# A decoder layer on one core: side steps in four units instead of three, some additions moved to GpSimd, and four score matmuls ahead of a key tile's maxima

## What is computed

```python
x = x + self_attention(layernorm(x))             # 2 heads of 64, rotary, causal
x = x + cross_attention(layernorm(x), context)   # 16 heads of 8, 1601 keys per batch element
x = x + feed_forward(layernorm(x))               # 128 -> 512 -> 128, exact gelu

def feed_forward(x, W1, b1, W2, b2, scale):      # per batch element
    lt = x[1:17]; even, odd = lt[::2], lt[1::2]
    m1 = (even[:4, :, None] * odd[:4, None, :]).reshape(512, 128)
    m2 = (even[4:, :, None] * odd[4:, None, :]).reshape(128, 512)
    h = gelu(x @ (W1 + scale * m1).T + b1)
    return h @ (W2 + scale * m2).T + b2
```

## Time and profile before

| | us |
|---|---|
| median of 3 runs | 508.89 |
| the profiled execution | 505.43 |
| its span, first to last instruction | 503.4 |
| TensorE busy | 412.4 (82%) |
| VectorE busy | 351.8 (70%) |
| ScalarE busy | 299.2 (59%) |
| GpSimd busy | 58.7 (12%) |
| mean granted TensorE clock | 0.875 of full |

### The profile page before, as it was taken

How to read it: one execution, slowest core, us unless ns; L and a number is a source line. 1 busy time by engine, 2 the same in 40 slices (tenths; PEclk the granted TensorE clock), 3 DMA queues, 4 the chain that set the end, 5 groups by cost and what they waited for, 6 DMA issues and landing times.

```text
span 503.4 us, 9677 instructions
## 1 busy us (share of the span) xinstructions
PE 412.4 (82%) x3680; PEld 188.0 (37%) x3680; DVE 351.8 (70%) x821; ACT 299.2 (59%) x624; POOL 58.7 (12%) x55
## 2 busy tenths in 40 slices
PE   1753889989769879989779879989779879999946
PEld 1541123445223334555223333545223333433324
DVE  2742988895659976695769976694769977895041
ACT  1411038777447756876557756767557747899811
POOL 3500000270000000190000000190000000000000
PEclk9957559999779997998889998998889988999955
DMA  6063640043033020224033020224033020000000
GB/s 234 1 216 118 195 121 2 1 147 101 10 107 97 3 78 2 76 99 148 2 116 97 2 78 1 77 100 147 1 121 92 5 75 0 12 3 3 1 0 10
DMA packets 19100, 33.96 MB, mean 67 GB/s; under 512 B 1527, under 2 KB 16599, under 8 KB 19055
## 3 DMA queue, kind: packets, MB, share of 16 engines
q1 hardware_dynamic: 19054, 33.36, 20.6%
HBM read 17.58 MB, written 11.93 MB: 59 GB/s over the span
## 4 chain that ended last, share of the span: by engine, by line
PE 42%; DVE 35%; ACT 8%; DMA 6%; issue 5%; SPq 2%; POOL 1%; POOLq 0%; ACTq 0%; DVEq 0%
DVE part_max L531 21%; PE wsum L858 11%; PE ring L889 8%; PE score L873 5%; ACT probs L729 4%; DMA q_rows<-q_parts 2%; PE ring L1020 2%; PE ring L1032 2%; PE ring L925 2%; PE ring L1025 2%; PE ring L914 2%; DMA ctx_sb<-ctx_t 2%; PE ring L979 2%; DMA q_unit<-consts 1%; PE ring L1012 1%
## 5 line engine op out<-in xcount | busy, mean ns | idle before, releaser
L531 DVE TENSOR_REDUCE part_max<-ring 128x1 f32<-128x401 f32 x512 | 257.1, 566 | 63.8 <-PE ring L889 63.2
L729 ACT ACTIVATE probs<-score 128x512 f32<-128x512 f32 (+1 forms) x416 | 222.4, 596 | 75.3 <-PE score L873 74.2
L889 PE MATMUL ring<-k_unit,q_unit 51*128 51x401 bf16 x512 | 162.5, 372 | 37.4 <-DMA q_unit<-consts 17.0
L858 PE MATMUL wsum<-probs,v_unit 128*32 128x256 f32 (+1 forms) x1664 | 142.1, 416 | 3.8 <-ACT unit_ctx L734 3.4
L873 PE MATMUL score<-q_unit,k_unit 51*128 51x256 bf16 (+1 forms) x832 | 129.2, 290 | 1.8 <-ACT probs L729 0.5
L889 PEld LDWEIGHTS ring<-k_unit,q_unit 51*128 51x128 bf16 x512 | 48.6, 96 | 150.7 <-issue 62.2
L858 PEld LDWEIGHTS wsum<-probs,v_unit 128*32 128x32 f32 (+1 forms) x1664 | 34.3, 111 | 53.9 <-issue 40.0
L873 PEld LDWEIGHTS score<-q_unit,k_unit 51*128 51x128 bf16 (+1 forms) x832 | 49.5, 98 | 12.9 <-ACT probs L729 8.9
L740 ACT ACTIVATE q_unit<-ring 3x512 bf16<-3x512 bf16 x32 | 18.7, 584 | 30.4 <-PE ring L900 30.2
L501 POOL TENSOR_TENSOR var<-mv,c_sb 128x2 f32<-128x2 f32 x4 | 0.8, 195 | 237.4 <-DVE mv L666 237.4
L914 PE MATMUL ring<-c_sb,xn 128*128 128x128 f32 x24 | 6.9, 384 | 24.9 <-DVE xn L567 10.0
(11 more groups left out here) (103 smaller groups left out, 330.2 us busy)
## 6 DMA issues: line engine op xcount, KB each, us to landing
k_unit<-k_rows SPq DMA_DIRECT2D x32, 300.2 KB
v_unit<-v_aug SPq DMA_DIRECT2D x16, 234.0 KB, 5.9
ctx_sb<-ctx_t SPq DMA_DIRECT2D x4, 800.5 KB, 5.6
...
```

What stands on the lines that cost most here:

```text
L531: v_.tensor_reduce(part_max[:, par, q, head, hp, c:c + 1], ring[s][:, 0:CW], AX.X, ALU.max)\
L729: a_.activation(probs[0:rows, i % PB, :], score[i % EB][0:rows, :], ACT.Exp)\
L858: last = mm(wsum[32 * j:32 * j + 32, 0:S], v_unit[0:rows, u, VQ * t + VW * j:VQ * t + VW * j + 32], probs[0:rows, i % PB, S * (j // 2):S * ...
L889: mm(ring[s][:, 0:CW], q_unit[rows, u, hp, P * q:P * (q + 1)], k_unit[rows, u, L * hp + (CW - 1) * c:L * hp + (CW - 1) * c + CW], start=Tr ...
```

## The change

1. One table, SIDE, replaces the four; it names side steps at 31 tiles of all four units, each step after the tile's maxima and in front of its value product. COUNT replaces PAIRS, AHEAD goes from (4, 16, 14, 8) to (8, 16, 8, 8).
2. A tile's four score matmuls come first, the two of one half, then the two of the other; then all its maxima. The half is chosen so that the first maxima matmul is on the half of the last scores.
3. sel, L1 and L2 go. SyncE writes the sixteen normalised tokens to DRAM and reads the eight even ones back into all 128 partitions; GpSimd multiplies them by the columns of the odd ones (xn3_t) and adds the weights (item low).
4. Three additions go from VectorE to GpSimd: the rotated q and k, x1 with bo, x2 with b2.
5. The context of the element after is loaded right behind V3 (item ctx), unit 1 of the next element with "load". The split of q becomes an item of its own, two tiles behind q.

```diff
+SIDE = {
+    (0, 0): [("prep", "K0")], (0, 2): [("prep", "K1")], (0, 3): [("prep", "ln1")], (0, 5): [("prep", "xT")],
+    (0, 6): [("post", "OT")], (0, 7): [("prep", "qk")], (0, 8): [("prep", "qks"), ("post", "Wo")],
+    (0, 11): [("prep", "e0"), ("prep", "e1"), ("post", "ln3")], (0, 12): [("prep", "K2")],
+    (1, 0): [("prep", "soft")], (1, 1): [("post", "x3T"), ("prep", "K3")], (1, 2): [("prep", "v")],
+    (1, 3): [("prep", "pT0"), ("prep", "pT1")], (1, 4): [("prep", "store0")], (1, 5): [("prep", "av")],
+    (1, 7): [("prep", "aT")], (1, 9): [("prep", "wo")], (1, 10): [("post", "low")],
+    (1, 12): [("prep", "store1"), ("prep", "ln2")],
+    (2, 1): [("prep", "x2T")], (2, 3): [("prep", "q")], (2, 4): [("prep", "V0")], (2, 5): [("prep", "split")],
+    (2, 6): [("prep", "V1")], (2, 8): [("prep", "V2")], (2, 10): [("prep", "V3")], (2, 12): [("prep", "load")],
+    (3, 0): [("ctx", 2)], (3, 2): [("post", "h0")], (3, 5): [("post", "h1")], (3, 8): [("post", "out")],
 }
...
-AHEAD = (4, 16, 14, 8)
-PAIRS = ((1, 1, 1, 1, 1, 1, 2, 1, 1, 1, 1, 1, 2), (1,) * 13,
-         (1, 1, 1, 2, 1, 1, 1, 2, 1, 1, 1, 1, 0), (2, 2, 1, 2, 2, 1, 2, 2, 1, 2, 2, 1, 2))
-TURN_AT = (10, 10, 11, 10)
-PV_AT = {t: (t - 2,) for t in range(KT)}
...
+            "av", "aT", "store1", "wo", "ln2", "x2T", "q", "split", "V0", "V1", "V2", "V3", "load"]
+POST_ALL = ["OT", "Wo", "ln3", "x3T", "low", "h0", "h1", "out"]
+
+
+
+AHEAD = (8, 16, 8, 8)
+COUNT = ((3, 3, 2, 1, 2, 3, 2, 2, 1, 2, 1, 1, 1), (3, 3, 3, 2, 3, 2, 3, 3, 2, 2, 2, 2, 2),
+         (3, 2, 3, 2, 3, 1, 2, 3, 2, 3, 3, 3, 2), (3, 3, 3, 3, 3, 3, 3, 3, 3, 3, 3, 3, 4))
+TURN_AT = (10, 11, 11, 10)
+
+
+def max_head(k):
+
+    return 1 - k % 2
...
-    assert len(todo) == 2 * sum(PAIRS[u])
-    todo = [item for item in todo if item[1] < UNITS]
+    assert len(todo) == sum(COUNT[u])
     plan = []
     for t in range(KT):
-        pairs = PAIRS[u][t]
-        for n in range(2):
-            plan += todo[:min(pairs, 1)]
-            todo = todo[min(pairs, 1):]
-            plan.append(("S", v, t, n))
-        plan += todo[:2 * pairs - 2] if pairs > 1 else []
-        todo = todo[2 * pairs - 2:] if pairs > 1 else todo
+        now, todo = todo[:COUNT[u][t]], todo[COUNT[u][t]:]
+        now = [item for item in now if item[1] < UNITS]
+        first = 1 - max_head(now[0][2]) if now else 0
+        for n, par in enumerate((first, 1 - first)):
+            plan.append(("S", v, t, n, 0, par))
+            plan.append(("S", v, t, n, 1, par))
+        plan += now
         if t == 3 and v:
             plan.append(("norm", v - 1))
-        plan += [("prep", name, b + 1) for name in PREP_MID.get((u, t), []) if b + 1 < B]
-        plan += [("post", name, b - 1) for name in POST_MID.get((u, t), []) if b]
-        for at in PV_AT.get(t, ()):
-            if at >= 0:
-                plan.append(("PV", v, at))
-            elif v:
-                plan.append(("PV", v - 1, KT + at))
         if t == TURN_AT[u] and v + 1 < UNITS:
             plan.append(("mT", v + 1))
-        plan += [("prep", name, b + 1) for name in PREP_END.get((u, t), []) if b + 1 < B]
-        plan += [("post", name, b - 1) for name in POST_END.get((u, t), []) if b]
+        for kind, what in SIDE.get((u, t), []):
+            at = b + {"prep": 1, "post": -1, "ctx": 2}[kind]
+            if 0 <= at < B:
+                plan.append((kind, what, at))
+        if t >= 2:
+            plan.append(("PV", v, t - 2))
+        elif v:
+            plan.append(("PV", v - 1, KT - 2 + t))
     assert not todo
     return plan
...
+START_PLAN = ([("prep", name, 0) for name in PREP_ALL] + [("ctx", 2, 1)] + [("M", 0, k) for k in range(MU)] +
+              [("mT", 0)] + [("M", 1, k) for k in range(AHEAD[1])])
...
+                if kind == "norm" and item[1] % UB == 3 and item[1] < UNITS - 1:
+                    b = item[1] // UB
+                    load_unit(b + 1, 2)
+                    load_unit(b + 1, 3)
+                elif kind == "ctx":
+                    s, n = RING["prep", "V3", item[2] - 1]
+                    sp.wait_ge(drained[s], n + 1)
+                    sp.dma_start(ctx_sb[:, 0:L], ctx_t[item[2], :, :]).then_inc(ctx_in, 16)
...
+                elif kind == "post" and item[1] == "x3T":
+                    b = item[2]
+                    sp.wait_ge(xn3_done, b + 1)
+                    sp.dma_start(ffn_rows[b, :, :], xn3[1:17, 0, :]).then_inc(rows_out, 16)
+                    sp.wait_ge(rows_out, 16 * (b + 1))
+                    if b:
+                        sp.wait_ge(add_done, 8 * b)
+                    sp.dma_start(even[:, :, :], ffn_rows[b, 0:16:2, :].unsqueeze(0).to_broadcast([P, 8, D]))\
+                        .then_inc(even_in, 16)
...
+                        g.tensor_tensor(x1_bo[:, b, :, :], x1[:, :, :],
+                                        W("bo").unsqueeze(1).to_broadcast([P, QT, D]), ALU.add).then_inc(x1_bo_set, 1)
+                    elif name == "qks":
+                        for part in ("qk", "qks"):
+                            s, n = RING["prep", part, b]
+                            pool.wait_ge(drained[s], n + 1)
+                        g.tensor_tensor(qk_rot[:, :], rope_a[:, :], rope_b[:, :], ALU.add).then_inc(qk_done, 1)
...
+                    g.tensor_tensor(x2_b2[:, :, :], x2[:, :, :],
+                                    W("b2").unsqueeze(1).to_broadcast([P, QT, D]), ALU.add).then_inc(x2_b2_set, 1)
+                elif kind == "post" and item[1] == "low":
+
+                    b = item[2]
+                    pool.wait_ge(even_in, 16 * (b + 1))
+                    s, n = RING["post", "x3T", b]
+                    pool.wait_ge(drained[s], n + 1)
+                    for i in range(4):
+                        g.tensor_scalar(w1_add[:, D * i:D * (i + 1)], even[:, i, :], xn3_t[:, 2 * i + 2:2 * i + 3],
+                                        W("scale"), ALU.mult, ALU.mult).then_inc(add_done, 1)
+                    for i in range(4):
+                        g.tensor_scalar(w2_add[:, :].rearrange("p (r i j) -> p r i j", r=4, i=4)[:, :, i, :],
+                                        even[:, 4 + i, :].rearrange("p (j r) -> p r j", r=4),
+                                        xn3_t[:, 2 * i + 10:2 * i + 11], W("scale"), ALU.mult, ALU.mult)\
+                            .then_inc(add_done, 1)
+                    pool.wait_ge(add_done, 8 * b + 4)
+                    g.tensor_tensor(w1_all[:, :], w1_add[:, :], W("W1"), ALU.add).then_inc(low_done, 1)
+                    pool.wait_ge(add_done, 8 * b + 8)
+                    g.tensor_tensor(w2_all[:, :], w2_add[:, :], W("W2"), ALU.add).then_inc(low_done, 1)
...
+            def scores(v, t, n, hp, par):
+
+                u, i = v % UB, score_index(v, t, n)
                 keys = P if t < KT_FULL else LAST
                 rows = slice(HALF * par, HALF * par + KR)
-                if t == 0 and par == 0:
-                    s, n = RING["mT", v]
-                    pe.wait_ge(drained[s], n + 1)
-                if i >= EB:
+                if t == 0 and n == 0 and hp == 0:
+                    s, m = RING["mT", v]
+                    pe.wait_ge(drained[s], m + 1)
+                if hp == 0 and i >= EB:
                     pe.wait_ge(probs_done, i - EB + 1)
-                for hp in range(2):
-                    last = mm(score[i % EB][0:keys, S * hp:S * (hp + 1)],
-                              k_unit[rows, u, L * hp + P * t:L * hp + P * t + keys], q_unit[rows, u, hp, :],
-                              start=True, stop=True)
-                last.then_inc(scores_ready, 1)
+                last = mm(score[i % EB][0:keys, S * hp:S * (hp + 1)],
+                          k_unit[rows, u, L * hp + P * t:L * hp + P * t + keys], q_unit[rows, u, hp, :],
+                          start=True, stop=True)
+                if hp == 1:
+                    last.then_inc(scores_ready, 1)
...
                 elif name in ("h0", "h1"):
-                    s = take(item, ("x3T", "L1"))
+                    pe.wait_ge(low_done, 2 * pb + 1)
+                    s = take(item, ("x3T",))
                     for j in (2 * int(name[1]), 2 * int(name[1]) + 1):
                         last = mm(ring[s][:, S * (j % 2):S * (j % 2 + 1)], w1_all[:, P * j:P * (j + 1)], xn3_t[:, :],
                                   start=True, stop=True)
                     last.then_inc(filled[s], 1)
                 elif name == "out":
-                    s = take(item, ("L2", "h0", "h1"))
+                    pe.wait_ge(low_done, 2 * pb + 2)
+                    s = take(item, ("h0", "h1"))
```

More of the change, by code:

```diff
@@ L182 @@
 PLAN = START_PLAN + [item for v in range(UNITS) for item in unit_plan(v)] + END_PLAN
[L183 removed]
+ORDER = {item[1:3] + item[5:]: item[3] for item in PLAN if item[0] == "S"}
+NO_SLOT = ("ln1", "ln2", "ln3", "soft", "store0", "store1", "split", "low", "load")
 def ring_slots():
```

101 lines of the change are left out of this document (24 added, 77 removed), and 3 rows, old and new, of the table PREP_END.

## The result

The changed kernel takes 472.9 us (median of 4 runs, 466.9 to 476.9) against 507.76 before: a ratio of 0.928, 95% interval 0.916 to 0.939. One of the four executions, 476.9 us, fell in a slower state of the chip and is left out of the ratio. I forecast 463, range 438 to 486, and faster by over 2% with 0.95. The profiled execution took 471.9, its span 470.1.

What follows compares the result with a forecast made beforehand. No engine was full: TensorE, the largest, was busy 86% of a full batch, with clock missing. Start 69 + 95 + 2 x 97 + 72 + end 28 = 458 us span, 460 with the time around it, 463 as median; range 438 to 486.

Steps and rivals of the forecast that it cites:

- Units at 97 to 99% where nothing stalls, 77% where steps crowd: Units fill their busiest engine 97 to 99% with main work only, 77% in unit 2 where dependent side steps crowd.
- I take 1.00 in the batches: Clock in the batches: gaps of 1 to 3 us go, so it rises from an average of 0.92 to 1.00.
- What would show it: Trace signs: batches 94 to 100 us, units within 3 us, clock over 0.97, six more table loads, end 27 to 30.
- (b): Rival, better packed: the queue makes up for the order, TensorE 84, occupancy 0.95, 435 us; chance 0.13.
- ScalarE's tables, +2.6 us a batch: Splitting h0 and h1 makes four table loads of two, +2.6 us of ScalarE; TensorE's wait lies inside the occupancy taken.
- Four scores first, +5.2 us a batch: Score and maxima matmuls in each tile pair differently: TensorE 32.8 us against 27.6; bounds 0 and +19.4.
- Low-rank matrices, 3.8 and 3.6 us a batch taken off two engines: Selection and its products leave TensorE (3.8 us), copies, scalings and additions leave VectorE (3.6); GpSimd's work is hidden in batches.
- The end, +1.9 us: From xn3 to the first hidden matmul 10.1 us against 7.8, less 0.4 leaving the chain; end 28 us.
- Rival (a): Stalls stay: dependent steps, in-order queues and doubled table loads keep occupancy at 86%, the clock falls; 482 us, chance 0.17.
- (d): Rival, no overlap: score pairs on one half in a row end the overlap, TensorE 103; 516 us, chance 0.03.
- (e): Rival, slower: the same in place, ring and score buffers freed later, occupancy 86%, 120 us a batch; 545 us, chance 0.02.
- (c): Rival, GpSimd slow in the end: +12.8 us there rather than +1.9; 474 us, chance 0.05.

Runs made afterwards that it cites:

- Spreading alone: Kernel before with the new side-step tables and maxima counts; old tile order, additions on VectorE, sel, L1 and L2 on TensorE: 486.0 us (0.951).
- best version: Changed kernel with old tile order, four Gelus together, q and its split earlier in unit 2, last element's W1 part on VectorE: 444.5 us (0.880).
- the repeat: The changed kernel run again, nothing edited, beside other follow-ups on the same chip: 471.7 us (0.928 of the kernel before).

## Why the prediction was right, and where its terms were off

- *Units at 97 to 99% where nothing stalls, 77% where steps crowd*: held. Spreading alone gave 25 of the 35 us, and the units of the changed kernel without a stall have TensorE busy 94 to 95%. The 92% taken for the busiest engine was met too: 93% in batch 2 and 91% in batch 1 (95.3 of 104.4), but at a lower clock, which made the same matmuls longer.
- *"I take 1.00 in the batches" for the clock*: of all steps this one failed, and it is most of the 12 us by which the span is longer than forecast. The clock averaged 0.92 in batch 1 and 0.97 in batch 2. Behind it stands the price of 0 for the queries' wait, "still covered": the store of the queries and the loads behind it took 8.5 and 6.7 us in batches 1 and 2 and not two times 2.1 plus issue, so TensorE waited 2.8 and 1.0 us, and in batch 1 the clock fell. A wait of 1.4 us at a table load did the same in unit 3 of both. In the best version, with the queries asked for one and two tiles earlier, unit 2 takes 21.8 us in both full batches. The prediction also read the earlier trace rows too simply where it says that each such gap is followed by the lower level: in that unit the value products take 1.08 us behind the waits of 1.3 and 2.7 us and stay at 0.64 behind the one of 1.1.
- *What would show it*: of the signs of being right, batch 1 missed 94 to 100 us and its 104.4 is just over the 104 named as a sign of being wrong (101.2 in the repeat); the units of a batch lie 8 to 9 us apart and not 3, with the feed-forward's unit the longest; batch 1's clock is under 0.97; the end is 26.75 for 27 to 30. The time from the first score to the value product, 0.67, lies between (b)'s 0.6 and the 0.71. The six further table loads came, at 1.28 us.
- *ScalarE's tables, +2.6 us a batch, "inside the occupancy"*: too small where it hurts. In the last unit four loads stand in 23 us, of which ScalarE is busy 18.6; putting the Gelus together was worth 5 us in all, more with the old order (0.916 to 0.895, 10 us). The rule of ScalarE: Activation LUTs, section "Table sets: the hidden batching unit", of the Trainium skill, to batch activation calls by set, was right in direction. The 2.66 us a switch in ScalarE: Activation LUTs, section "What ACT_TABLE_LOAD costs", of the Trainium skill was not seen: the load took 1.28 and the Exp started 1.29 after the load's start, as the Gelu did 1.30 after it in the earlier trace rows.
- *Additions to GpSimd, 2.7 us a batch off VectorE*: 1.6, since L581's 1.85 us had shrunk before it moved. With the steps spread it stands no longer beside GpSimd's split of the keys, and where it stays on VectorE in the new order it takes 0.69 us in all four elements.
- *Four scores first, +5.2 us a batch*: with 2.5 in the last batch that is 13 us, or 18 if batch 0 pays as well; 6 to 8 us were measured by undoing it alone, about 12 with the Gelus together (0.919 to 0.895). The sign is right, the pairing model is not: 0.67 us and not 0.71 for three maxima, and 0.66 in the old order. What it costs stands beside side steps.
- *Low-rank matrices, 3.8 and 3.6 us a batch taken off two engines*: the size as TensorE's work was right, its worth was not. It was worth nothing in the old order (a wait for GpSimd) and 16 us or more in the new one, some 5 more than its work. That the clock behind the matmuls of 4 rows makes up this rest is likely: it averaged 0.81 to 0.85 in the three units that held them and 1.00 without. In the kernel before no clock was lost behind them.
- *The end, +1.9 us*: it is 0.75 longer between the two profiles, but the end varies: 24.0 to 26.0 us in three traces with the old end, 26.7 to 26.9 in most and up to 29.4 in those with the new one. So +1.9 is about right. From xn3 (450.16) to the first hidden matmul 10.2 us, forecast 10.1:

```profile
450.19 0.33 SPq L455 DMA_DIRECT2D ffn_rows<-xn  x1
...
451.55 0.36 SPq L459 DMA_DIRECT2D even<-ffn_rows  x1
455.23 1.73 POOL L540 TENSOR_SCALAR w_add<-even,xn_t,w_sb 128x128 f32<-128x128 f32 x4 [5.41 <-DMA even<-ffn_rows]
456.94 2.17 POOL L543 TENSOR_SCALAR w_add<-even,xn_t,w_sb 128x128 f32<-128x128 f32 x4
459.08 1.26 POOL L548 TENSOR_TENSOR w_all<-w_add,w_sb 128x512 f32<-128x512 f32 x1
...
460.39 3.78 PE L1029 MATMUL ring<-xn_t,w_all 128*128 128x256 f32 x8 [9.49 <-POOL w_all L548]
...
465.30 2.02 PE L1037 MATMUL ring<-w_all,hidden 128*128 128x128 f32 x16 [1.13 <-ACT hidden L830]
```

  The write and the read take 5.0 us together (I had 6.2), the multiplications 0.43 and 0.54 each (0.35), the addition 1.26 (1.1). L1037 then ran at full clock, 2.0 us; the same product took 3.75 in the profiled end before.
- *Rival (a)*, the stalls stay, had the right places, unit 2 and the tables; its 482 was 9 us too high, as my 463 was 10 too low, and TensorE was busy 91 to 93% and not 86. (d) and (e) fell, since the halves of the rows pair up in every order. (b) had the pairs packed as before, which holds in plain tiles, but fell by the time, 38 us below the measured one. (c) fell with the 10.2 us.
- *Luck*: the order inside the tile was priced some 5 to 12 us too high and the low-rank part some 5 too low. Both errors make the forecast too long, and the clock and the waits, which it left out, make it too short. Without them 463 would have been further off.
